# A pipeline of linear attention written out for all pairs of heads, and gate products placed in four column groups

## The chip, the cores and the metric

The kernel runs on one core of one Trainium2 chip. A core has TensorE (PE: matrix products, with a queue of its own for weight loads, PEld), VectorE (DVE), ScalarE (ACT), GpSimd (POOL) and SyncE (SP, which here only issues DMAs). The metric is device time in microseconds of the whole program, the median of several runs; lower is better. Durations come from one profiled execution.

## The reference

The input x is 4 sequences of 512 tokens with 256 channels, float32. Four layers are computed one after the other, each added to x:

```python
x = x + attn_a(layernorm(x))      # softmax attention, 16 heads of 16
x = x + ffn(layernorm(x))         # stage b
x = x + attn_b(layernorm(x))      # gated linear attention, 16 heads of 128
x = x + ffn(layernorm(x))         # stage d
```

The linear attention projects to q, k, v and a gate, runs a causal convolution with four taps over q and k, a silu and a layer norm for each head, and then the recurrence `S = (1 - b) S + b v k^T`, `o = S q`, which the kernel computes in blocks with a decay matrix:

```python
q = silu(causal_dwconv(h @ Wq)); k = silu(causal_dwconv(h @ Wk)); v = h @ Wv
q = layernorm(q); k = layernorm(k); b = sigmoid(h @ Wb + bb); gate = silu(h @ Wg)
# for every token t: S = (1 - b_t) S + b_t v_t k_t^T ; o_t = S q_t
out = (o * gate) @ Wo
```

The feed-forward layer picks two of eight routes for each token, and adds the token's result, times the route's gate, to **row number route** of the output. Only rows 0 to 7 of the first sequence get anything:

```python
h = silu(silu(x @ w1.T) @ w3.T) @ w2.T
for k in range(2):
    out = out.at[indices_k[:, k]].add(gates[:, k:k+1] * h)   # indices are 0..7
```

So the sum over tokens can be taken before the last product: gates^T (8 x 2048) times the hidden values (2048 x 256), and that times w2.

## The kernel before

The stages follow each other with a barrier of all engines between them: softmax attention, its projection, feed-forward b, layer norm and decay (c), linear attention, feed-forward d. Semaphores by hand order all work; nothing is scheduled by a tool.

**Linear attention** (`linear_attention`). Work goes by units: a unit is one head on one sequence. A pair of heads has `BODY` = 8 units, there are 8 pairs and 64 units. Each engine runs a function `step(pair, k, u, of)` for each unit, in which the phases of several units interleave: TensorE turns the normed q and k of unit u-2 back (L1340), projects q and k of unit u (L1306), turns the convolved rows of u-1 (L1333), projects the gate (L1306), computes scores of u-2 (L1325), the read-out of u-3 (L1392, L1389), projects values (L1319) and multiplies the gated rows of u-5 with Wo (L1414). DVE does the convolution steps (L1513), statistics (L1543), masks (L1518), the gated rows (L1563), values (L1569), the decay scans (L1522) and the sum into `x_tok` (L1532). ACT does the first tap, silu, norms and the high parts of split operands; POOL does the small sums of the norm and the low parts. SP loads the decay rows `keep` of each unit and, in a pair's second unit, the next pair's weights.

The helper `steps` writes the first two pairs out on every engine, and then a loop on the engine (`eng.Fori`) whose body is two pairs. With `last_apart` (SP, POOL, ACT, DVE) the loop runs for pairs 2 to 5, twice, and the last two pairs are written out; TensorE loops over pairs 2 to 7, three times. Within a loop the counts that `wait` (L1161) and `wait_apart` (L1167) wait for, and the columns of `par`, `beta_tok` and `wo` that depend on the head, come from registers that the engine's sequencer computes.

**Feed-forward** (`norm_and_ffn`, run for b and d). TensorE works out the router's logits (`rows`, 8 partitions, L773), turns them (L780), makes the upper products (L793) and the middle ones (L805); ACT writes the results of silu into `hidden_t` and `hidden`. DVE picks the two routes and makes the gates (L896 to L934). When `gates_ready` comes, TensorE multiplies, for each of the 16 token tiles, the gates (128x8) with `hidden` (128x256) into `rows`, L833. DVE copies that out (`summed`, L936), TensorE turns it with two transposes (L837), DVE copies (L938), TensorE multiplies with w2 (L841), DVE adds to `x_tok` (L940), and in d SP stores the eight rows. In b, POOL splits the weights of the first heads meanwhile (`ahead`).

A float32 product (not the split kind, float32r) shows as two passes with two weight loads in the trace: L833 is 16 products in the program and 32 in the trace.

## Time and profile before

| | |
|---|---|
| median of 3 runs | 1269.4 us (1269.29 to 1273.27) |
| the profiled execution | 1268.87 us |
| its span, first to last instruction | 1267.1 us |
| PE busy | 1172.9 us (93%) |
| DVE busy | 969.6 us (77%) |
| ACT busy | 758.1 us (60%) |
| POOL busy | 569.5 us (45%) |
| linear attention | 388.6 to 1209 us |
| feed-forward b, d | 316 to 375 us, 1209 to 1267 us |

Busy time counts no register, branch or semaphore instructions and no issuing of DMAs. Busy shares are means over stages with different limits, so they don't say what a stage waits for. Where TensorE is busy all the time, the distance from one unit's start to the next tells what it loses; in the timeline a number in brackets is idle time of that engine just before the row, and the name behind it is what ended it. Matmuls overlap: the start of one is about 0.12 (256 columns) or 0.23 us (512) after the last one's, though each takes longer.

### The profile page before, as it was taken

How to read it: one execution, taken by the hardware profiler on the slowest of the kernel's cores; microseconds unless marked ns; L12 is line 12 of the kernel's file. 1: busy time of each engine (PE TensorE's matmuls, PEld its weight loads, DVE VectorE, ACT ScalarE, POOL GpSimd, SP SyncE). 2: the span in 40 equal slices, each digit the busy share in tenths (PEclk: the TensorE clock that was granted, in tenths of full speed). 3: DMA queues.
4: the chain of work that ended last, by engine and by line, in shares of the span. 5: the costliest groups of instructions: out<-in, count | busy, mean ns of one | idle time of the engine just before them, and what ended most of it. 6: DMA issues, size and time to landing. Idle time of an engine off the chain costs nothing. (4 is left out here: it accounts for less than half of the span.)

```text
span 1267.1 us, 22205 instructions
## 1 busy us (share of the span) xinstructions
PE 1172.9 (93%) x7062; PEld 915.1 (72%) x7062; DVE 969.6 (77%) x2038; ACT 758.1 (60%) x1400; POOL 569.5 (45%) x1066
## 2 busy tenths in 40 slices
PE   4799999998787999999999999999999999999778
PEld 3343434335555889898998988898898999899655
DVE  6767677764625888888898898888898988989451
ACT  3156565674334676776766676676767676666323
POOL 5100000000711675676676675676576666656410
PEclk9589999999799999999999999999999999999889
DMA  4212222200301111102011111201110110101020
GB/s 148 66 43 52 54 47 58 50 17 1 116 1 65 39 38 59 39 26 72 27 38 39 59 39 29 71 26 39 59 39 27 72 38 27 38 26 39 1 67 1
DMA packets 26677, 56.66 MB, mean 45 GB/s; under 512 B 5367, under 2 KB 10359, under 8 KB 25399
## 3 DMA queue, kind: packets, MB, share of 16 engines
q1 hardware_dynamic: 26551, 55.11, 14.4%
q8 instruction: 63, 1.03, 0.3%
q14 instruction: 63, 0.52, 0.1%
HBM read 39.95 MB, written 2.29 MB: 33 GB/s over the span
## 5 line engine op out<-in xcount | busy, mean ns | idle before, releaser
L555 DVE TENSOR_REDUCE a_neg_max<-a_scores 128x1 f32<-128x512 f32 x236 | 154.9, 685 | 64.1 <-PE a_scores L359 63.9
L1513 DVE SCALAR_TENSOR_TENSOR l_conv<-l_proj_q,par,l_conv 128x511 f32<-128x511 f32 (+2 forms) x192 | 142.5, 742 | 55.2 <-ACT l_conv L1430 52.0
L497 ACT ACTIVATE a_probs<-a_scores_t 128x1024 f32<-128x1024 f32 x128 | 124.3, 1023 | 57.9 <-PE a_scores_t L374 56.8
L1436 ACT ACTIVATE l_conv<-l_conv,par 128x512 f32<-128x512 f32 x128 | 92.4, 723 | 101.4 <-DVE l_conv L1513 101.0
L1513 DVE SCALAR_TENSOR_TENSOR l_conv<-l_proj_k,par,l_conv 128x511 f32<-128x511 f32 (+2 forms) x192 | 142.9, 744 | 6.3 <-DVE l_conv L1513 0.6
L1522 DVE TENSOR_TENSOR_SCAN l_decay<-l_keep,l_diag 128x256 f32<-128x256 f32 (+1 forms) x256 | 146.1, 633 | 0.0
L1249 POOL TENSOR_TENSOR l_k_tok<-l_normed,k_norm 128x256 f32<-128x256 f32 x64 | 56.3, 880 | 157.9 <-ACT l_normed L1447 157.9
L86 POOL MEMSET ln_minus_half_b<- 128x4 f32 x1 | 0.1, 101 | 281.0 <-POOLq L611 281.0
L359 PE MATMUL a_scores<-a_k_stack,a_q_stack 48*128 48x512 f32 x236 | 108.7, 507 | 15.3 <-DVE a_neg_max L555 11.7
L359 PEld LDWEIGHTS a_scores<-a_k_stack,a_q_stack 48*128 48x128 f32 x236 | 42.7, 193 | 105.9 <-DVE a_neg_max L555 87.4
L1447 ACT ACTIVATE l_normed<-l_turn_q,l_shift,l_scale 128x128 f32<-128x128 f32 x256 | 96.3, 457 | 21.1 <-POOL l_shift L1241 21.1
L1239 POOL TENSOR_TENSOR l_scale<-l_small,l_minus_half 128x8 f32<-128x8 f32 x64 | 105.0, 1641 | 5.0
L1392 PE MATMUL l_outp<-l_masked,l_values 128*128 128x128 f32 (+1 forms) x512 | 105.8, 330 | 0.9 <-DVE x_tok L1532 0.9
L1447 ACT ACTIVATE l_normed<-l_turn_k,l_shift,l_scale 128x128 f32<-128x128 f32 x256 | 97.1, 480 | 0.0
L1280 POOL TENSOR_TENSOR l_gated_lo<-l_gated,l_gated_hi 128x512 fp32r<-128x512 f32 x64 | 82.2, 1285 | 9.9 <-ACT l_gated_hi L1470 9.9
L1319 PE MATMUL l_proj_gv<-head_hi,xn_hi 128*128 128x256 f32 x256 | 83.5, 326 | 2.1 <-ACT l_gate L1489 2.1
L1489 ACT ACTIVATE l_gate<-l_proj_gv 128x512 f32<-128x512 f32 x64 | 38.2, 597 | 77.7 <-PE l_proj_gv L1306 77.6
L374 PE MATMUL a_scores_t<-a_q_stack,a_k_stack 50*128 50x512 f32 x256 | 72.3, 447 | 6.5 <-DMA a_q_stack<-a_max_lo 5.5
L1414 PE MATMUL l_outp<-wo_hi,l_gated_hi 128*128 (+1 forms) x256 | 72.9, 285 | 4.9 <-DVE l_gated L1563 3.1
L1392 PEld LDWEIGHTS l_outp<-l_masked,l_values 128*128 128x128 f32 x512 | 73.1, 193 | 4.5 <-issue 1.0
L1569 DVE TENSOR_TENSOR l_values<-l_proj_gv,beta_tok 128x512 f32<-128x512 f32 x64 | 44.2, 691 | 39.3 <-PE l_proj_gv L1319 39.1
L1414 PE MATMUL l_outp<-wo_hi,l_gated_lo 128*128 (+1 forms) x256 | 71.6, 280 | 0.0
(292 smaller groups left out, 3429.8 us busy)
## 6 DMA issues: line engine op xcount, KB each, us to landing
l_keep<-keep_rows SPq DMA_DIRECT2D x64, 384.0 KB, 3.4
head_raw<-w_heads SPq DMA_DIRECT2D x8, 1024.0 KB, 6.4
a_q_stack<-a_dense_hi SPq DMA_DIRECT2D x64, 64.0 KB, 2.2
a_k_stack<-a_dense_hi SPq DMA_DIRECT2D x64, 64.0 KB, 2.2
x_tok<-x SPq DMA_DIRECT2D x4, 512.0 KB, 7.0
a_q_stack<-a_dense_lo SPq DMA_DIRECT2D x32, 64.0 KB, 2.2
a_k_stack<-a_dense_lo SPq DMA_DIRECT2D x32, 64.0 KB, 2.2
wo_raw<-w_o SPq DMA_DIRECT2D x1, 2048.0 KB, 11.6
```

Of the source, the lines that this page charges most:

```text
L359: pe.matmul(max_bank(g, j), half_rows(q_stack[i], e, STACK)[:, slot, t * P:(t + 1) * P], half_rows(k_stack[i], e, STACK)[:, slot, :], star ...
L497: act.activation(probs[:, n % 2, 2 * half:2 * half + 2, :], scores_t[half][:], ACT.Exp, scale=SOFT_SCALE).then_inc(probs_done, 1)
L555: dve.tensor_reduce(neg_max[:, g % 2, at:at + 1], max_bank(g, j), AX.X, ALU.max, negate=True).then_inc(max_done, 1)
L1239: pool.tensor_tensor(scale[:, i, :], small[:, 7, :], minus_half[:], ALU.pow).then_inc(scales_ready, 1)
L1280: pool.tensor_tensor(gated_lo[:, k % 4, :], gated[:], f32(gated_hi[:, k % 4, :]), ALU.subtract).then_inc(gated_lo_done, 1)
L1319: last = pe.matmul(proj_gv[:, t * PAIR:(t + 1) * PAIR], lhs, rhs, start=(j == 0), stop=(j == 3 * KD - 1))
L1392: last = pe.matmul(outp[:, i * P:i * P + WIDTH[i]], values[:, c % 2, i, e * DK:(e + 1) * DK], masked[:, m, START[i]:START[i] + WIDTH[i]], ...
L1414: last = pe.matmul(outp[:, t * D:(t + 1) * D], lhs, rhs, start=(j == 0), stop=(j == 5))
L1436: act.activation(conv[:, w, m, :], conv[:, w, m, :], ACT.Silu, bias=par[:, h, 2 * TAPS + w:2 * TAPS + w + 1]).then_inc(act_sem[w], 1)
L1447: last = act.activation(normed[:, w, t, :], turn[w][:, t * P:(t + 1) * P], ACT.Identity, scale=scale[:, m, j:j + 1], bias=shift[:, m, j:j ...
L1513: ins = dve.scalar_tensor_tensor(conv[:, w, m, s:], proj[w][:, 0:SEQ - s], par[:, h, tap:tap + 1], conv[:, w, m, s:], ALU.mult, ALU.add)
L1522: last = dve.tensor_tensor_scan(decay[:, START[i]:START[i] + WIDTH[i]], keep[:, r, i * P:i * P + WIDTH[i]], diag[:, 0:WIDTH[i]], 0.0, ALU. ...
```

## The change

**No loop in the linear attention.** `steps` calls `step` for all eight pairs in turn on every engine, so pair and unit are plain numbers: all counts that are waited for and all column offsets are constants. The work, its order on each engine and the semaphores stay.

**Gate products in four column groups.** The last gate sum is written into a new tile `slots`, 32 columns for each token tile, of which 8 hold the gates and 24 are zero (POOL zeroes the tile early). The product of token tile t writes to 32 output partitions that start at 32 x (t mod 4) of a PSUM bank `sums` with 128 partitions, in place of partitions 0 to 7; each group sums four tiles. DVE copies all 128 partitions, and in place of the two transposes TensorE multiplies with `fold` (128x8, ones where the partition is e, e+32, e+64 or e+96), which turns and adds the four groups in one. DVE makes `fold` from the unit matrix ahead of the routing. The router's logits use the first 8 partitions of `sums` as they did `rows`.

```diff
--- before.py
+++ after.py
@@ -715,13 +715,16 @@
         ratio = sb("ratio", [P, NT])
         total = sb("total", [P, NT])
         weight = sb("weight", [P, 2, NT])
-        gates = sb("gates", [P, 3, NT, NE])
-        summed = sb("summed", [NE, D])
+        gates = sb("gates", [P, 2, NT, NE])
+        slots = sb("slots", [P, NT, SLOT])
+        fold = sb("fold", [P, NE])
+        summed = sb("summed", [P, D])
         summed_t = sb("summed_t", [P, KD, NE])
         xt = [[psum(f"xt{k}", [P, SEQ]) for k in range(KD)]]
         up = [psum(f"up{i}", [P, SEQ]) for i in range(2)]
         mid = [psum(f"mid{i}", [P, 2, D]) for i in range(2)]
-        rows = psum("rows", [NE, SEQ])
+        sums = psum("sums", [P, SEQ])
+        rows = sums[0:NE, :]
         turned = psum("turned", [P, (NT + KD) * NE])
         logits_ps = turned[:, 0:NT * NE].rearrange("p (t e) -> p t e", e=NE)
         tail = turned[:, NT * NE:].rearrange("p (k e) -> p k e", e=NE)
@@ -729,10 +732,10 @@
 
         names = ("w_loaded", "rank_set", "w_hi_ready", "w_lo_ready", "router_done", "router_read", "logits_done", "route",
                  "gap_ready", "ratio_ready", "gates_ready", "up_done", "up_read", "mid_done", "mid_read", "acc_done",
-                 "summed_ready", "tail_done", "tail_read", "rows_done", "rows_added", "stored")
+                 "summed_ready", "tail_done", "tail_read", "rows_done", "rows_added", "stored", "slots_set", "fold_ready")
         (w_loaded, rank_set, w_hi_ready, w_lo_ready, router_done, router_read, logits_done, route,
          gap_ready, ratio_ready, gates_ready, up_done, up_read, mid_done, mid_read, acc_done,
-         summed_ready, tail_done, tail_read, rows_done, rows_added, stored) = (sem(n) for n in names)
+         summed_ready, tail_done, tail_read, rows_done, rows_added, stored, slots_set, fold_ready) = (sem(n) for n in names)
         block = ctx.enter_context(nc.Block())
 
         @block.sync
@@ -754,6 +757,7 @@
             ln.constants(pool)
             for g in range(NB):
                 ln.deviations(pool, g)
+            pool.memset(slots[:], 0.0).then_inc(slots_set, 1)
 
             for e in range(NE):
                 pool.memset(rank[:, e:e + 1], float(NE - e)).then_inc(rank_set, 1)
@@ -770,7 +774,7 @@
                     pe.wait_ge(router_read, g)
                 for k in range(KD):
                     for lhs, rhs in split_passes(w_in_hi[:, k, D:], w_in_lo[:, k, D:], xn_hi[:, k, tok], xn_lo[:, k, tok]):
-                        last = pe.matmul(rows[:], lhs, rhs, start=(j == 0), stop=(j == 3 * KD - 1))
+                        last = pe.matmul(rows, lhs, rhs, start=(j == 0), stop=(j == 3 * KD - 1))
                         j += 1
                 last.then_inc(router_done, 1)
 
@@ -830,11 +834,14 @@
             for t in range(NT):
                 if t % 2 == 0:
                     pe.wait_ge(mid_read, t // 2 + 1)
-                last = pe.matmul(rows[:, 0:D], gates[:, 2, t, :], hidden[:, t, :], start=(t == 0), stop=(t == NT - 1))
+                j = t % (P // SLOT)
+                last = pe.matmul(sums[j * SLOT:(j + 1) * SLOT, 0:D], slots[:, t, :], hidden[:, t, :],
+                                 start=(t < P // SLOT), stop=(t >= NT - P // SLOT))
             last.then_inc(acc_done, 1)
+            pe.wait_ge(fold_ready, 1)
             pe.wait_ge(summed_ready, 1)
             for k in range(KD):
-                last = pe.transpose(tail[:, k, :], summed[:, k * P:(k + 1) * P], ident[0:NE, 0:NE])
+                last = pe.matmul(tail[:, k, :], summed[:, k * P:(k + 1) * P], fold[:], start=True, stop=True)
             last.then_inc(tail_done, 1)
             pe.wait_ge(tail_read, 1)
             for k in range(KD):
@@ -851,7 +858,7 @@
                 act.wait_ge(router_done, g + 1)
                 if g >= 2:
                     act.wait_ge(logits_done, g - 1)
-                act.activation(logit_rows[:, g % 2, :], rows[:], ACT.Copy).then_inc(router_read, 1)
+                act.activation(logit_rows[:, g % 2, :], rows, ACT.Copy).then_inc(router_read, 1)
 
             copy_logits(0)
             ln.high_parts(act, 1)
@@ -891,6 +898,8 @@
                 if g + 2 < NB:
                     ln.statistics(dve, g + 2)
             ln.low_parts(dve, NB - 1)
+            dve.tensor_reduce(fold[:], ident[:].rearrange("p (j e) -> p e j", e=SLOT)[:, 0:NE, :], AX.X,
+                              ALU.add).then_inc(fold_ready, 1)
             dve.wait_ge(logits_done, NB)
             dve.wait_ge(rank_set, NE)
             dve.tensor_copy(logits[:], logits_ps).then_inc(route, 1)
@@ -931,9 +940,10 @@
                 dve.tensor_tensor(gates[:, pick, :, :], chosen[:, pick, :, :],
                                   weight[:, pick, :].unsqueeze(2).to_broadcast(wide), ALU.mult).then_inc(route, 1)
             dve.wait_ge(route, step + 5)
-            dve.tensor_tensor(gates[:, 2, :, :], gates[:, 0, :, :], gates[:, 1, :, :], ALU.add).then_inc(gates_ready, 1)
+            dve.wait_ge(slots_set, 1)
+            dve.tensor_tensor(slots[:, :, 0:NE], gates[:, 0, :, :], gates[:, 1, :, :], ALU.add).then_inc(gates_ready, 1)
             dve.wait_ge(acc_done, 1)
-            dve.tensor_copy(summed[:], rows[:, 0:D]).then_inc(summed_ready, 1)
+            dve.tensor_copy(summed[:], sums[:, 0:D]).then_inc(summed_ready, 1)
             dve.wait_ge(tail_done, 1)
             dve.tensor_copy(summed_t[:], tail).then_inc(tail_read, 1)
             dve.wait_ge(rows_done, 1)
@@ -1178,19 +1188,11 @@
 
             return not isinstance(u, int) or 0 <= u - lag < UNITS
 
-        def steps(eng, step, lags, last_apart=False):
-
-            for pair in range(2):
+        def steps(step, lags):
+
+            for pair in range(PAIRS):
                 for k in range(BODY):
-                    step(pair, k, pair * BODY + k, pair)
-            with eng.Fori(1, PAIRS // 2 - 1 if last_apart else PAIRS // 2) as couple:
-                for of in range(2):
-                    for k in range(BODY):
-                        step(2 * couple + of, k, couple * (2 * BODY) + (of * BODY + k), of)
-            if last_apart:
-                for of in range(2):
-                    for k in range(BODY):
-                        step(PAIRS - 2 + of, k, (PAIRS - 2 + of) * BODY + k, of)
+                    step(pair, k, pair * BODY + k, pair % 2)
             for k in range(lags):
                 step(PAIRS, k, UNITS + k, 0)
 
@@ -1208,7 +1210,7 @@
                     wait(sp, w_ready, 4 * pair)
                     sp.dma_start(w_raw[:], w_heads[bass.ds(pair + 1, 1)]).then_inc(w_loaded, 16)
 
-            steps(sp, step, 0, last_apart=True)
+            steps(step, 0)
 
         @block.gpsimd
         def _(pool):
@@ -1293,7 +1295,7 @@
                 if k in SPLIT_AT and has_next(pair):
                     low_weights(pair, of, k - SPLIT_AT[0])
 
-            steps(pool, step, 4, last_apart=True)
+            steps(step, 4)
 
         @block.tensor
         def _(pe):
@@ -1418,7 +1420,7 @@
             def head_of(head, e):
                 return head + e
 
-            steps(pe, step, 6)
+            steps(step, 6)
 
         @block.scalar
         def _(act):
@@ -1498,7 +1500,7 @@
                     wait(act, read_out, v - 1)
                     act.activation(state[:, k % 2, :], score_b[:, 2 * P:2 * P + DK], ACT.Copy).then_inc(state_done, 1)
 
-            steps(act, step, 4, last_apart=True)
+            steps(step, 4)
 
         @block.vector
         def _(dve):
@@ -1579,7 +1581,7 @@
                     scan(kk % 2, range(TPB)).then_inc(decay_done, 1)
 
             dve.wait_ge(consts_set, 4)
-            steps(dve, step, 7, last_apart=True)
+            steps(step, 7)
 
 
 def build(nc, x, w_qkv, w_proj, b_proj, w_in, w_mid, w_out, w_beta, b_beta, w_heads, w_o, params, norms, k_norms, out):
```

The lines of the changed kernel are numbered a little higher than before (L1340 is L1342, L1513 is L1515, L833 is L838, L837 is L844).

TensorE at the end of the loop's body before: the products with Wo, then a register step and the branch back to the body's start, where the transposes of the normed q stand.

```order
L1414 MATMUL l_outp<-wo_hi,l_gated_hi 128x256
L1414 MATMUL l_outp<-wo_lo,l_gated_hi 128x256
L1414 MATMUL l_outp<-wo_hi,l_gated_lo 128x256
L1186 REGISTER_ALU
L1186 COMPARE_AND_BRANCH
```

The same place in the changed kernel:

```order
L1416 MATMUL l_outp<-wo_hi,l_gated_hi 128x256
L1416 MATMUL l_outp<-wo_lo,l_gated_hi 128x256
L1416 MATMUL l_outp<-wo_hi,l_gated_lo 128x256
L1342 MATMUL l_turn_q<-ident,l_normed 128x128 x4
L1308 MATMUL l_proj_q<-xn_hi,head_hi 128x512
L1308 MATMUL l_proj_q<-xn_lo,head_hi 128x512
```

The products and the transposes follow each other directly; register step and branch are gone.

DVE in the loop before, from one unit's sum into `x_tok` on (`ISA` and `REGISTER_ALU` are register instructions of the sequencer, which compute a column offset or a count):

```order
L1161 REGISTER_ALU
L1532 TENSOR_TENSOR x_tok<-l_outp,x_tok 128x512
L1161 REGISTER_ALU
L1513 ISA
L1513 SCALAR_TENSOR_TENSOR l_conv<-l_proj_q,par,l_conv 128x511
L1161 ISA
L1513 ISA
L1513 SCALAR_TENSOR_TENSOR l_conv<-l_proj_q,par,l_conv 128x510
L1161 ISA
L1543 BN_STATS l_stats<-l_turn_q 128x6 x4
L1543 BN_STATS l_stats<-l_turn_k 128x6 x4
L1161 REGISTER_ALU
```

The same unit's work in the changed kernel:

```order
L1534 TENSOR_TENSOR x_tok<-l_outp,x_tok 128x512
L1515 SCALAR_TENSOR_TENSOR l_conv<-l_proj_q,par,l_conv 128x511
L1515 SCALAR_TENSOR_TENSOR l_conv<-l_proj_q,par,l_conv 128x510
L1545 BN_STATS l_stats<-l_turn_q 128x6 x4
L1545 BN_STATS l_stats<-l_turn_k 128x6 x4
L1515 SCALAR_TENSOR_TENSOR l_conv<-l_proj_q,par,l_conv 128x509
```

The vector work and its order are the same, without register instructions in between.

TensorE at the end of stage d, before and then changed:

```order
L805 MATMUL f_mid_d<-w,f_hidden_t_d 128x256 x16
L833 MATMUL f_rows_d<-f_hidden_d,f_gates_d 8x256 x16
L837 MATMUL f_turned_d<-ident,f_summed_d 128x8 x2
L841 MATMUL f_rows_d<-w,f_summed_t_d 8x256 x2
```

```order
L809 MATMUL f_mid_d<-w,f_hidden_t_d 128x256 x16
L838 MATMUL f_sums_d<-f_hidden_d,f_slots_d 32x256 x16
L844 MATMUL f_turned_d<-f_fold_d,f_summed_d 128x8 x2
L848 MATMUL f_sums_d<-w,f_summed_t_d 8x256 x2
```

The gate products write 32 partitions instead of 8, and the transposes of `summed` with `ident` are products of `summed` with `fold`.

## Rows read from the trace of the kernel before

**Rows 1.** Page, head: the span of the profiled execution.

```profile
span 1267.1 us, 22205 instructions
```

**Rows 2.** Busy time by stretch: us, busy of each engine (count), granted clock, DMA.

```profile
578.00:777.00 199.00, 198.58 (x1296) 179.34 (x1295) 174.92 (x371) 139.24 (x286) 131.06 (x248) 1.00 0.13 44
```

**Rows 3.** Timeline, PE: first projection product of units 8, 16, 17, 32, 48, 63.

```profile
482.36 0.48 PE L1306 MATMUL l_proj_q<-xn_hi,head_hi 128*128 128x512 f32 x1
...
580.33 0.48 PE L1306 MATMUL l_proj_q<-xn_hi,head_hi 128*128 128x512 f32 x1
...
593.25 0.48 PE L1306 MATMUL l_proj_q<-xn_hi,head_hi 128*128 128x512 f32 x1
...
779.84 0.47 PE L1306 MATMUL l_proj_q<-xn_hi,head_hi 128*128 128x512 f32 x1
...
979.09 0.47 PE L1306 MATMUL l_proj_q<-xn_hi,head_hi 128*128 128x512 f32 x1
...
1162.80 0.48 PE L1306 MATMUL l_proj_q<-xn_hi,head_hi 128*128 128x512 f32 x1
```

**Rows 4.** PE at the back edges; then queue instructions of line L1186: min/median/max.

```profile
777.29 0.27 PE L1414 MATMUL l_outp<-wo_hi,l_gated_lo 128*128 x1
779.43 0.65 PE L1340 MATMUL l_turn_q<-ident,l_normed 128*128 128x128 f32 x4 [1.87 <-issue]
...
978.68 0.65 PE L1340 MATMUL l_turn_q<-ident,l_normed 128*128 128x128 f32 x4 [1.65 <-issue]
...
L1186 PEldq COMPARE_BRANCH  x3: 83/3288/3501, 775.8 to 1173.0; - x3
```

**Rows 5.** Timeline, DVE and PE: convolution steps in loop, written out; a product with Wo.

```profile
587.83 1.64 DVE L1513 SCALAR_TENSOR_TENSOR l_conv<-l_proj_k,par,l_conv 128x510 f32<-128x510 f32 x2 [0.15 <-DVE l_conv L1513]
...
985.29 2.30 DVE L1513 SCALAR_TENSOR_TENSOR l_conv<-l_proj_k,par,l_conv 128x511 f32<-128x511 f32 x3
...
591.37 0.38 PE L1414 MATMUL l_outp<-wo_hi,l_gated_hi 128*128 x1 [0.39 <-DVE l_gated L1563]
```

**Rows 6.** Timeline: tail of stage d, gate products and what stands around them.

```profile
1255.37 0.29 DVE L934 TENSOR_TENSOR f_gates_d<-f_gates_d 128x128 f32<-128x128 f32 x1
1255.42 1.08 ACT L875 ACTIVATE f_hidden_d<-f_mid_d 128x512 f32<-128x512 f32 x2
1255.72 7.07 PE L833 MATMUL f_rows_d<-f_hidden_d,f_gates_d 128*8 128x256 f32 x32 [0.32 <-DVE f_gates_d L934]
1262.83 0.41 DVE L936 COPY f_summed_d<-f_rows_d 8x256 f32<-8x256 f32 x1 [7.16 <-PE f_rows_d L833]
...
1263.30 0.28 PE L837 MATMUL f_turned_d<-ident,f_summed_d 8*128 8x8 f32 x2 [0.51 <-DVE f_summed_d L936]
```

**Rows 7.** Timeline: gate products of stage b, and POOL behind the barrier.

```profile
365.03 7.07 PE L833 MATMUL f_rows_b<-f_hidden_b,f_gates_b 128*8 128x256 f32 x32 [0.32 <-DVE f_gates_b L934]
...
375.91 0.30 POOL L978 MEMSET d_zeros<- 16x256 f32 x1 [24.32 <-POOLq L1631]
```

**Rows 8.** Timeline, PE: a context product of softmax attention; its line, min/median/max ns.

```profile
122.63 1.07 PE L391 MATMUL a_ctx_acc<-a_probs,a_v_tok 128*32 128x512 f32 x8
123.62 0.49 PE L359 MATMUL a_scores<-a_k_stack,a_q_stack 48*128 48x512 f32 x2
...
L391 PE MATMUL a_ctx_acc<-a_probs,a_v_tok x512: 589/617/1061, 63.3 to 295.5; 128*32 128x512 f32 x171
```

**Rows 9.** Timeline: a four-pass product, a copy from PSUM, DVE ahead of routing.

```profile
574.98 0.61 PE L1373 MATMUL l_score_b<-l_values,l_k_tok 128*128 128x128 f32 x4
...
386.33 0.39 DVE L1035 COPY beta_tok<-d_turned 128x256 f32<-128x256 f32 x1
...
1245.55 0.29 DVE L896 COPY f_logits_d<-f_turned_d 128x128 f32<-128x128 f32 x1 [10.04 <-PE f_turned_d L780]
```

**Rows 10.** DMA queues, the larger one for instructions: packets, MB, share of engines.

```profile
q8 instruction: 63, 1.03, 0.3%
```

**Rows 11.** Busy time by stretch, near the end of the linear attention.

```profile
1190.00:1195.00 5.00, 5.00 (x20) 4.46 (x19) 1.12 (x2) 0.28 (x1) 1.12 (x1) 0.51 0.00 0
```

## The prediction

> **What bounds the kernel now.** I read the span and the busy shares first, then the busy time of each engine in two pairs of the linear attention, then when TensorE starts each unit, then the rows around the places that the edit touches. The span is 1267.1 us and the profiled execution 1268.87 us, so 1.8 us lie outside the span [rows 1]. In the linear attention TensorE is busy 198.58 of 199 us at the full clock, DVE 174.92, ACT 139.24 and POOL 131.06 [rows 2]. So here the end is set by TensorE, and what counts is the time that TensorE loses, not what others save.
>
> What it loses is read from the start of each unit's first projection product. Units 8 to 16 start at 482.36 and 580.33: 97.97 us for 8, or 12.246 each. Units 48 to 63 start at 979.09 and 1162.80: 183.71 for 15, or 12.247 each [rows 3]. That is the undisturbed pace, the same in the first two pairs, which every engine has written out, and in the last two, where only TensorE still loops. Between them it is worse: units 16 to 32 take 779.84 - 580.33 = 199.51 us and units 32 to 48 take 979.09 - 779.84 = 199.25, where 16 units at that pace take 195.95.
>
> In the two feed-forward stages TensorE works alone at one place: the 16 gate products, which run as 32 passes one behind the other in 7.07 us, while DVE waits 7.16 for them and ACT has nothing after 1256.50 [rows 6]. It is the chain to the end in stage d, and to the barrier in stage b, where POOL had by then waited 24.32 us [rows 7].
>
> **The change, part 1: no loop.** It removes what lies between 195.95 and the measured: 199.51 + 199.25 - 2 x 195.95 = **6.86 us**, and I can name what it consists of.
> - The two taken back edges. From the last product of the loop's body to the next pass 777.29 to 779.43 = 2.14 us go by, where such products follow each other in 0.12; TensorE is idle 1.87 and at the second edge 1.65 [rows 4]. TensorE's queue spends 3288 and 3501 ns on the branch (median and longest of three; the third, 83 ns, is the one that falls through), of which the queued products hide the rest. The first edge costs 2.14 - 0.12 = 2.02, the second 0.22 less by its idle row, 1.80: together 3.8 us.
> - The late vector work. In the loop DVE has register instructions ahead of each convolution step, and 0.15 us go by idle between two of them (587.83); in the last two pairs three run on without a gap (985.29). So DVE ends its chain later, and TensorE waits for the gated values: 0.39 us at 591.37, in a unit that takes 593.25 - 580.33 = 12.92 instead of 12.25 [rows 3, 5]. It comes at the first units of a pair, 0.25 to 0.67 us at a time, eight times: the rest, 3.0 us.
>
> What is late next when both are gone? Nothing, as far as 23 units with DVE, ACT and POOL written out show (8 to 15, and 48 to 62): they hold 12.25 each. The one thing that these rows don't cover is TensorE without a loop after unit 16. Bounds: at least the branches, 3.8; at most 7.5, since the first units of each pair could have been held even at 12.25. I take 6.9. Queue instructions (register work on all queues) go too; TensorE's engine doesn't feel them. No DMA is moved: SP issues the same transfers on the same counts.
>
> The row on the branch meets two pages of the Trainium skill. "Advanced Engine Details and Errata", Control Flow Timing, gives about 108 ns for a compare-and-branch: by that the back edge would hide wholly behind queued products and this part would be worth 3.0. "Runtime: NRT & Kernel Launch", Instruction fetch mechanics, says that a taken branch to a target outside the small window of fetched pages has to fetch it first: by that the whole 3.8 is gone. The trace agrees with the second (3288 ns).
>
> **Part 2: gate products in four column groups.** Sixteen products, two passes each, now go to four groups of 32 output partitions. The only such work in the trace is the context product of the softmax attention: 8 passes of 512 columns in 1.07 us from the first start to the last end, one pass 0.589 at least, so the last starts 0.48 after the first, where two rounds of four start 0.46 apart plus a skew of 0.02 [rows 8]. Passes of four groups therefore do run side by side, a round of 512 columns taking 0.46. For 256 columns: one pass behind the other is (7.07 - 0.38) / 31 = 0.216 [rows 6]; a round is 0.23 (half of 0.46) to 0.25 (0.216 plus the 0.03 by which a 512-column round exceeds two passes of 0.216). I take 0.24. Eight rounds: 7 x 0.24 + 0.02 + 0.38 = 2.1 us. Saved: 7.07 - 2.1 = **5.0 us** per stage. The upper bound is that, the lower nothing, if groups don't overlap here.
> - Does another wait take its place? The last quarter needs ACT's last gated rows, at 1255.42 + 1.08 = 1256.50. It would start at 1255.72 + 6 x 0.24 = 1257.2 [rows 6]. So no, with 0.7 us to spare.
> - The two transposes of 0.28 us become two 128-row products with the fold matrix, four passes with 128-column weights. Nearest rows: four passes of 128x128 in 0.61 [rows 9]; the transposes themselves, 0.28 [rows 6]. So +0 to +0.33; I take +0.3, since the weights are as wide as in the row of 0.61.
> - The copy out of PSUM has 128 partitions instead of 8: 0.39 for 128x256 against 0.41 [rows 6, 9]. Nothing.
> - The fold sum on DVE is one small reduction just ahead of a wait of 10.04 us [rows 9]: hidden. DVE waits for one more semaphore ahead of the last gate sum, long given, and writes in strides: 0 to 0.1, taken as 0. The zeroing on POOL (512 columns; 256 took 0.30 [rows 7]) stands ahead of the rank constants and, in b, of the weight split that ended 24 us before the barrier: hidden; without that cover some 0.6.
>
> Per stage 5.0 - 0.3 = 4.7, two stages **9.4 us**. Bounds -0.8 to 10.
>
> "TensorEngine Tiling (Array Packing)" of the Trainium skill, Key Properties, speaks against this part: changing the tiling mode drains TensorE. The trace shows how little: the plain products start 123.62, that is 1.0 after the first of the grouped passes and before the last ends, and here DVE's copy stands behind the switch anyway. By the rule the sum stays as it is, within 0.2.
>
> **Sum.** 6.9 + 9.4 = 16.3. 1268.9 - 16.3 = 1252.6 for a profiled execution; that one stood 0.5 under the median of 1269.4, so **1253.1 us**.
>
> **Rivals.**
> - The clock moves. The changed tails shift everything behind them, and stretches at 1.2 GHz (0.51 granted at 1190 to 1195 [rows 11]) follow idle ones. Such a stretch of 5 us costs 2.5, one half as long 1.25. One more: 1254.4 to 1255.6. One less: 1250.6 to 1251.9. The start of the linear attention and both feed-forward tails are places for it. Against much more: TensorE is at 1.00 through all of the middle [rows 2].
> - Only the branch was the loop's doing, and the slow first units of a pair have another cause: 1253.1 + 3.0 = 1256.1. Against: units 48 to 63 have none.
> - The groups don't overlap for these products, the change does not do what it says: 1253.1 + 2 x 5.0 = 1263. Against: [rows 8], the same types and rows; only half the columns and back-to-back quarters are new.
> - Slower: straight code has to be fetched too. The larger queue for instructions moved 63 packets in the span [rows 10]; the six pairs that the edit writes out take 595 of 1267 us, so by their share some 30. If each stalled TensorE, the change loses from 16.3 / 30 = 0.54 us each on; at the 1.9 us of a back edge it would be 1253 + 57 = 1310. Against: units 8 to 16 and every loop body are straight code, and show 12.246.
>
> **How the numbers follow.** Forecast as summed 0.68; a low clock stretch more 0.10, one less 0.08; slow units stay 0.06; groups don't overlap 0.05; fetch stalls 0.03. The range takes in both clock cases, the slow units and the bounds of the pass costs (0.5 either way): 1249.8 to 1257.2. About 0.3% is what a measurement of this kernel can tell from no change (4 us). Faster by more holds in all but fetch stalls: 0.96; within 0.3% 0.02, half of a mild fetch case; slower 0.02.
>
> **What would show it.** Right: no branch in TensorE's queue, no idle row of 1.87 or 1.65; units 16 to 48 in 391.9 us instead of 398.8; DVE's convolution steps without the 0.15; the 32 gate passes in 2.1 us in one row, DVE's wait before the copy about 2.2; the fold products at 0.6. Wrong if a unit after the 16th takes over 12.3, if the gate passes take over 3 us, or if a stretch with a low clock appears where none was.

## The result

The changed kernel takes 1253.7 us in the median (1252.24 to 1254.71), beside 1269.35 us for the kernel before (1269.02 to 1273.27): 0.987 of the time, with a 95% interval from 0.985 to 0.989. The forecast was 1253.1. The profiled execution after is 1253.70 us against 1268.87.

The page's head, and the stretch of the linear attention that [rows 2] shows of before (us, busy time of each engine with its count, granted clock, DMA share, GB/s):

```profile
span 1251.7 us, 21457 instructions
```

```profile
578.00:777.00 199.00, 199.00 (x1301) 180.23 (x1300) 178.31 (x375) 139.99 (x284) 131.90 (x252) 1.00 0.14 45
```

TensorE now has no idle time in these 199 us. The first projection products of units 16 and 48, to be read as [rows 3]:

```profile
576.46 0.48 PE L1308 MATMUL l_proj_q<-xn_hi,head_hi 128*128 128x512 f32 x1
...
968.35 0.48 PE L1308 MATMUL l_proj_q<-xn_hi,head_hi 128*128 128x512 f32 x1
```

They are 391.89 us apart, or 12.247 a unit; before it was 979.09 - 580.33 = 398.76. From unit 6 on no unit is over 12.3 (a unit's time here is the distance from the start of the unit ahead of it to its own). DVE's two convolution steps over k now run on without the 0.15 us of [rows 5]:

```profile
582.66 1.52 DVE L1515 SCALAR_TENSOR_TENSOR l_conv<-l_proj_k,par,l_conv 128x511 f32<-128x511 f32 x2
```

The tail of stage d, to be held against [rows 6]:

```profile
1244.68 0.29 DVE L944 TENSOR_TENSOR f_slots_d<-f_gates_d 128x128 f32<-128x128 f32 x1
1244.72 1.09 ACT L882 ACTIVATE f_hidden_d<-f_mid_d 128x512 f32<-128x512 f32 x2
...
1245.03 1.93 PE L838 MATMUL f_sums_d<-f_hidden_d,f_slots_d 128*32 128x256 f32 x32 [0.32 <-DVE f_slots_d L944]
1247.03 0.42 DVE L946 COPY f_summed_d<-f_sums_d 128x256 f32<-128x256 f32 x1 [2.06 <-PE f_sums_d L838]
...
1247.60 0.58 PE L844 MATMUL f_turned_d<-f_fold_d,f_summed_d 128*128 128x8 f32 x4 [0.64 <-DVE f_summed_d L946]
1248.22 0.17 DVE L948 COPY f_summed_t_d<-f_turned_d 128x16 f32<-128x16 f32 x1 [0.77 <-PE f_turned_d L844]
```

The 32 passes take 1.93 us instead of 7.07, and from their start to the end of the span it is 1251.7 - 1245.03 = 6.67 instead of 1267.1 - 1255.72 = 11.38. ACT's last gated rows are there at 1245.81, before the last quarter needs them. The same in stage b, where [rows 7] has 365.03 and 375.91:

```profile
364.60 1.93 PE L838 MATMUL f_sums_b<-f_hidden_b,f_slots_b 128*32 128x256 f32 x32 [0.32 <-DVE f_slots_b L944]
...
370.80 0.30 POOL L988 MEMSET d_zeros<- 16x256 f32 x1 [19.00 <-POOLq L1633]
```

From the gate products to the work behind the barrier it is 6.20 us instead of 10.88.

**Where 0.9 us of the expected gain went.** The gain in the span is 15.4 us, where 16.3 were summed. Two windows of the kernel after, and then two of the kernel before, at the same work (the end of stage c and the first unit of the linear attention), differ in the granted clock, the column behind the busy times:

```profile
382.00:388.00 6.00, 4.14 (x10) 3.30 (x11) 0.34 (x2) 0.69 (x1) 0.52 (x4) 0.51 0.57 151
388.00:398.00 10.00, 8.64 (x46) 7.08 (x45) 6.96 (x13) 5.20 (x7) 0.00 (x0) 0.95 0.24 98
```

```profile
387.00:393.00 6.00, 4.41 (x13) 3.50 (x13) 1.25 (x2) 0.69 (x1) 0.51 (x4) 0.72 0.57 187
393.00:403.00 10.00, 8.29 (x45) 6.48 (x43) 7.05 (x17) 5.52 (x8) 0.00 (x0) 1.00 0.18 76
```

The first row of each pair holds the end of TensorE's wait of 2.9 us for the barrier and the first products of unit 0. After, the clock stands at the lower level, 1.2 GHz, in all of it (0.51) and into the second; before, only through a part of the first (0.72). POOL's row behind b's barrier came 375.91 - 370.80 = 5.11 us earlier than before, unit 0 (383.86 against 388.59) 4.73, unit 6 (453.99 against 457.87) 3.88: 1.2 us of what b had saved are gone. Up to b's gate products the execution was 0.43 ahead. So 0.43 + 4.68 - 1.23 + 6.87 + 4.71 = 15.46, the 15.4 of the spans within rounding.

### The profile page after: what moved, and what is told of

Its sections match the earlier page's. It is cut to its first block and busy times, and to the rows that moved or that the text cites. A ratio compares the mean times of both kernels' runs of the same rounds, so it can differ in the third digit from the quotient of the medians.

```text
span 1251.7 us, 21457 instructions
## 1 busy us (share of the span) xinstructions
PE 1160.6 (93%) x7066; PEld 911.4 (73%) x7066; DVE 971.9 (78%) x2040; ACT 758.5 (61%) x1400; POOL 565.9 (45%) x1068
## 5 line engine op out<-in xcount | busy, mean ns | idle before, releaser
L1515 DVE SCALAR_TENSOR_TENSOR l_conv<-l_proj_q,par,l_conv 128x511 f32<-128x511 f32 (+2 forms) x192 | 142.5, 742 | 48.8 <-ACT l_conv L1432 46.5
L1515 DVE SCALAR_TENSOR_TENSOR l_conv<-l_proj_k,par,l_conv 128x511 f32<-128x511 f32 (+2 forms) x192 | 142.9, 744 | 4.6
L1251 POOL TENSOR_TENSOR l_k_tok<-l_normed,k_norm 128x256 f32<-128x256 f32 x64 | 52.1, 815 | 158.3 <-ACT l_normed L1449 158.3
L1416 PE MATMUL l_outp<-wo_hi,l_gated_hi 128*128 128x256 f32 x256 | 72.0, 281 | 4.1 <-DVE l_gated L1565 2.3
L1416 PE MATMUL l_outp<-wo_hi,l_gated_lo 128*128 128x256 f32 x256 | 71.7, 280 | 0.0
```

The lines of the kernel that those rows point to most:

```text
L1416: last = pe.matmul(outp[:, t * D:(t + 1) * D], lhs, rhs, start=(j == 0), stop=(j == 5))
L1515: ins = dve.scalar_tensor_tensor(conv[:, w, m, s:], proj[w][:, 0:SEQ - s], par[:, h, tap:tap + 1], conv[:, w, m, s:], ALU.mult, ALU.add)
```

## The experiments

The first is the kernel before with one half of the edit; all others are edits of the changed kernel, and those of the second part give single engines their loop back. No kernel leaves a part of the computation out. To free the comparison from what lies ahead of stage b, which moves by some microseconds from kernel to kernel (below), the profiled time less the start of b's gate products is used: 903.84 before, 889.10 after, -14.74. The time for units 16 to 48, from rows like those above, is called the middle.

The kernels on single engines and on the order of the groups ran once each, so of their whole times only large differences can be read:

| run | whole time | start of b's gate products | from there on |
|---|---|---|---|
| the changed kernel | 1253.70 | 364.60 | 889.10 |
| pe_loop | 1259.53 | 366.76 | 892.77 |
| short_branch | 1256.63 | 366.90 | 889.73 |
| dve_loop | 1255.40 | 365.94 | 889.46 |
| act_loop | 1251.73 | 363.36 | 888.37 |
| dve_act_loop | 1253.96 | 364.62 | 889.34 |
| four_loops | 1255.06 | 365.49 | 889.57 |
| two_groups | 1257.55 | 367.04 | 890.51 |
| groups_in_runs | 1264.58 | 369.62 | 894.96 |

The time from b's gate products on isn't steady either: from unit 63 to the gate products of stage d, with the same code, these nine take between 91.15 and 92.98 us. So the readings below rest on the middle and on single rows.

### Each half alone

**The loops gone, the gate products as before.**

```diff
-            steps(pe, step, 6)
+            steps(step, 6)
...
                 last = pe.matmul(rows[:, 0:D], gates[:, 2, t, :], hidden[:, t, :], start=(t == 0), stop=(t == NT - 1))
```

> The linear attention is written out on all engines, the feed-forward stages are those of before. Theory (the two halves are independent and add up): units 16 to 48 of TensorE take 391.9 us instead of 398.8, the gate products stay at 7.07 us, and the time is 1269.4 - 6.9 = 1262.5. Rival (the written-out code gives part back elsewhere, for example by fetching): over 1264, with units over 12.3 us after unit 16.

Measured: 1263.12 us (1261.85 to 1265.12), 0.9946 of the kernel before (0.9921 to 0.9972). Timeline, TensorE: units 16 and 48, and the gate products of d:

```profile
581.41 0.48 PE L1298 MATMUL l_proj_q<-xn_hi,head_hi 128*128 128x512 f32 x1
...
973.30 0.48 PE L1298 MATMUL l_proj_q<-xn_hi,head_hi 128*128 128x512 f32 x1
...
1249.99 7.07 PE L833 MATMUL f_rows_d<-f_hidden_d,f_gates_d 128*8 128x256 f32 x32 [0.32 <-DVE f_gates_d L934]
```

The middle is 391.89, as after. From b's gate products on the kernel takes 897.08: -6.76. The whole time, 0.6 over the 1262.5 expected, is still below the 1264 of the rival, and no unit after the sixteenth is over 12.3.

**The column groups, the loops as before.**

```diff
-            steps(step, 6)
+            steps(pe, step, 6)
...
                 last = pe.matmul(sums[j * SLOT:(j + 1) * SLOT, 0:D], slots[:, t, :], hidden[:, t, :],
...
```

> Gate products in four column groups, the linear attention with its loops as before. Theory: gate products 1.93 us in both stages, the linear attention keeps its idle rows of 1.87 and 1.65 at the back edges, time 1269.4 - 9.4 = 1260.0; up to 1.2 more if the start of the linear attention again has a longer stretch at 1.2 GHz, as in the changed kernel. Rival (the clock stretch comes from the loop half): then no longer stretch here and 1260.0 sharp.

Measured: 1261.02 us (1258.53 to 1263.29), 0.9927 (0.9903 to 0.9951). From b's gate products on 895.89: -7.95. With the loops' -6.76 that is -14.71, where both together have -14.74: the halves add up. (That they do so within 0.03 is luck in part. From unit 63 to d's gate products these four kernels happen to agree, 92.86 to 92.99.) The gate passes take 1.93 in both stages. The middle has its loop losses again, 975.93 - 576.96 = 398.97, the second back edge among them (timeline, TensorE):

```profile
576.96 0.48 PE L1316 MATMUL l_proj_q<-xn_hi,head_hi 128*128 128x512 f32 x1
...
975.52 0.65 PE L1350 MATMUL l_turn_q<-ident,l_normed 128*128 128x128 f32 x4 [1.75 <-issue]
975.93 0.47 PE L1316 MATMUL l_proj_q<-xn_hi,head_hi 128*128 128x512 f32 x1
```

The two windows at the start of the linear attention have the clock of the kernel after, not that of before:

```profile
382.00:388.00 6.00, 3.65 (x9) 2.91 (x10) 0.48 (x2) 0.66 (x1) 0.51 (x4) 0.56 0.48 118
388.00:398.00 10.00, 8.63 (x45) 7.00 (x44) 6.75 (x10) 5.24 (x8) 0.00 (x0) 0.92 0.29 118
```

So in these four kernels the 1.2 us go with this half: 2 x 4.7 less 1.2 is 8.2, and 7.95 are measured, with 0.2 of the rest in the middle (398.97 where the kernel before has 398.76). Kernels further down don't all keep to that.

### What the loop cost: which engine's

The kernels of this part give some engines the loop of the kernel before back, as `looped`, and leave the others written out.

**TensorE alone.**

```diff
-            steps(step, 6)
+            looped(pe, step, 6)
```

> The changed kernel, but TensorE alone runs pairs 2 to 7 in a loop, as before. Theory (the back edges cost 3.8 us, and the slow first units of a pair come from the other engines' register work): units 32 and 48 start 14.3 and 14.1 us after the one ahead, all others hold 12.25, time 1253.7 + 3.8 = 1257.5. Rival (TensorE's own registers make the slow units): units 17, 18, 25, 26 and so on take 12.5 to 12.9 too, 1260.6.

Measured: the middle is 397.56. Timeline of TensorE at the first back edge, windows around it, and the branch in TensorE's queue (minimum, median, maximum in ns):

```profile
774.20 0.27 PE L1432 MATMUL l_outp<-wo_hi,l_gated_lo 128*128 x1
776.36 0.69 PE L1358 MATMUL l_turn_q<-ident,l_normed 128*128 128x128 f32 x4 [1.88 <-issue]
776.77 0.71 PE L1324 MATMUL l_proj_q<-xn_hi,head_hi 128*128 128x512 f32 x1
```

```profile
770.00:776.00 6.00, 4.48 (x34) 4.12 (x32) 5.31 (x10) 3.80 (x10) 2.65 (x4) 1.00 0.03 5
776.00:781.00 5.00, 4.64 (x18) 3.83 (x19) 1.23 (x3) 2.52 (x4) 2.84 (x4) 0.66 0.19 67
781.00:787.00 6.00, 6.00 (x39) 5.35 (x38) 5.58 (x15) 2.31 (x5) 2.94 (x10) 1.00 0.04 15
```

```profile
L1196 PEldq COMPARE_BRANCH  x3: 83/3298/3515, 772.7 to 1170.2; - x3
```

Units 32 and 48 take 14.34 and 14.19, 4.03 more than 2 x 12.25; all others hold 12.25 but unit 33, with 13.84. That one goes with the clock, which stands at 0.66 from 776 to 781, right behind the idle 1.88 us. Whether that idle time brought the low clock is not shown: at the same edge of the kernel before, behind 1.87 us, the clock stays at 1.00 (779.5 to 784), and so it does here behind the second edge (976 to 980). So the edges alone cost 4.0, and the other slow units of [rows 3, 5] don't come from TensorE's loop alone.

**The branch without the distance.** TensorE has no loop over the work, but branches back twice over a single empty instruction at the same two places.

```diff
+                if short and pair in (4, 6):
+                    with short.Fori(0, 2) as turn:
+                        short.nop(nofuse=True)
```

> The changed kernel, with an empty loop of two turns put into TensorE's program ahead of pairs 4 and 6: two taken branches to a target a few instructions back. Theory (the 3.3 us of the branch are the fetch of a target far away): no idle of TensorE, 1253.7. Rival (any taken branch costs that much): TensorE is idle 1.6 to 1.9 us at units 32 and 48, 1257.5.

Measured: the middle is 391.89 with no idle time. The branch in TensorE's queue:

```profile
L1195 PEldq COMPARE_BRANCH  x4: 76/148/362, 774.0 to 970.3; - x4
```

The two taken ones need 219 and 362 ns, a branch with the same instruction over a whole loop body 3298 and more. It is the distance that costs, not the branch or the counter. One of the queues that move instructions agrees, which moves more where the target is far: 57 packets in the changed kernel, 63 with TensorE's loop alone, 58 with the short branch (page, DMA queues; packets, MB, share; pe_loop, then short_branch):

```profile
q8 instruction: 63, 1.03, 0.3%
```

```profile
q8 instruction: 58, 0.95, 0.3%
```

"Advanced Engine Details and Errata" of the Trainium skill, Control Flow Timing, gives some 108 ns for a compare-and-branch: the near ones here take 76 to 362 ns, the taken ones two to a little over three times that figure, and the far ones some thirty times. "Runtime: NRT & Kernel Launch", Instruction fetch mechanics, has a far target fetched first, and the trace agrees with it as far as these two kernels go.

**DVE alone; ACT alone; both; all but TensorE.**

```diff
-            steps(step, 7)
+            looped(dve, step, 7, last_apart=True)
```

> The changed kernel, but DVE alone loops over pairs 2 to 5, as before. Theory (DVE's register instructions ahead of each convolution step make the gated values late): the first two units of pairs 2 to 5 take 12.5 to 12.9 us again, 3.0 us in all, time 1256.7, with gaps of 0.15 us between convolution steps. Rival (ACT's registers do it): all units hold 12.25, 1253.7.

Measured: the middle is 971.44 - 577.86 = 393.58, 1.7 more, not 3.0. The same eight units as before are slow (17, 18, 25, 26, 33, 34, 41, 42), but at 12.39 to 12.46, with 12.69 once (34). The gaps are back (timeline, DVE):

```profile
585.23 1.64 DVE L1531 SCALAR_TENSOR_TENSOR l_conv<-l_proj_k,par,l_conv 128x510 f32<-128x510 f32 x2 [0.15 <-DVE l_conv L1531]
```

```diff
-            steps(step, 4)
+            looped(act, step, 4, last_apart=True)
```

> The changed kernel, but ACT alone loops over pairs 2 to 5, as before. Theory (DVE is the one that makes units slow): all units of TensorE hold 12.25 us, 1253.7. Rival (ACT's register work, 0.05 to 0.09 us ahead of its activations, makes DVE's chain late): the first two units of pairs 2 to 5 take 12.5 to 12.9, 1256.7.

Measured: 391.89 and no slow unit. ACT's register instructions alone cost nothing.

```diff
+            looped(act, step, 4, last_apart=True)
...
+            looped(dve, step, 7, last_apart=True)
```

> The changed kernel, but DVE and ACT both loop over pairs 2 to 5, as before. With DVE alone in a loop units 16 to 48 took 393.59 us, with ACT alone 391.89, written out 391.89, and the kernel before owed 3.0 us to its slow first units. Theory (DVE's and ACT's register work lie one behind the other on the chain from the first tap to the gated values, and ACT's shows only once DVE's has used the slack up): 394.9 us. Rival (the missing 1.3 us are POOL's or SP's registers): 393.6 us.

Measured: 394.17, 2.3 more; the eight units take 12.50 to 12.57. ACT's loop costs 0.6 where DVE is late too, and nothing without it. That reads like two chains that feed each other, each with a little slack; the slack itself was not measured.

```diff
+            looped(sp, step, 0, last_apart=True)
...
+            looped(pool, step, 4, last_apart=True)
...
+            looped(act, step, 4, last_apart=True)
...
+            looped(dve, step, 7, last_apart=True)
```

> The changed kernel, but SP, POOL, ACT and DVE loop over pairs 2 to 5, as before, and TensorE alone is written out. DVE and ACT in loops took 394.17 us for units 16 to 48, 0.7 short of the 3.0 that the slow units cost before, and it is units 17 and 33 that are short (12.57 and 12.55 instead of 12.91 and 12.87). Theory (POOL's or SP's register work brings the rest, at the first unit of an iteration): 394.8 us, units 17 and 33 at 12.9, time about 1256.6. Rival (TensorE's own loop brings it): 394.2 us, units 17 and 33 at 12.6, 1256.0.

Measured: 394.31, 2.4 more, with 12.57 at unit 17 and 12.65 at 33. With the column groups alone, where TensorE loops as well, these two take 12.90 and 12.89. So SP and POOL add 0.1. The middle of these four loops and the edges of TensorE's give 394.31 + 4.03 = 398.34, where the two kernels in which all five loop have 398.76 and 398.97: 0.4 to 0.6 are left that show only when TensorE loops with the others; neither TensorE alone nor the other four have them. What passes between them there stays open.

### The gate products: why 1.93

**Two groups in place of four.**

```diff
-                j = t % (P // SLOT)
+                j = t % 2
```

> The changed kernel with two column groups instead of four (even token tiles to partitions 0 to 31, odd ones to 32 to 63; copy and fold use 64 partitions). Theory (a round of passes of all groups takes one pass plus about 0.01 to 0.03 us, whatever the number of groups): 16 rounds of 0.22 to 0.23, so 3.6 to 3.9 us for the 32 passes in place of 1.93, and per stage 1.8 us more: 1253.7 + 3.6 = 1257.3. Rival (the passes are bound by the writing of results, not by the array): two groups take as long as four, 1253.7.

Measured (timeline, TensorE):

```profile
1247.46 3.65 PE L838 MATMUL f_sums_d<-f_hidden_d,f_slots_d 128*32 128x256 f32 x32 [0.32 <-DVE f_slots_d L944]
...
1251.72 0.58 PE L844 MATMUL f_turned_d<-f_fold_d,f_summed_d 64*128 64x8 f32 x4 [0.61 <-DVE f_summed_d L946]
```

Sixteen rounds of two: (3.65 - 0.38) / 15 = 0.218 a round, beside 0.216 for one pass alone [rows 6] and (1.93 - 0.38 - 0.02) / 7 = 0.219 for a round of four. With one, two or four groups a round costs what one pass costs. The fold of two groups takes the 0.58 us of four.

**Four groups, each filled before the next.** The four tiles of a group follow each other, where the changed kernel goes round the groups.

```diff
-                j = t % (P // SLOT)
+                j = t // (P // SLOT)
```

> The changed kernel, but token tiles 0 to 3 go to the first column group, 4 to 7 to the second and so on, in place of going round. Theory (products start in program order, so one that waits for its busy group holds up the next group's): hardly anything overlaps, the 32 passes take about 6.5 us, and the time is 1253.7 + 2 x 4.6 = 1262.9. Rival (each group has a queue of its own, since passes of four products start ahead of their second passes): 1.93 us as now, 1253.7.

Measured (timeline, TensorE):

```profile
1253.54 4.59 PE L838 MATMUL f_sums_d<-f_hidden_d,f_slots_d 128*32 128x256 f32 x32 [0.32 <-DVE f_slots_d L944]
```

That is neither the 7.07 of one behind the other (nor the 6.5 expected of a strict order) nor 1.93: theory and rival both miss. The passes start 0, 0.24, 0.46, 0.67, 0.89, 0.90, 1.11, 1.14, 1.32 and 1.35 us after the first, and so on in pairs up to the last four, which are single again: 4 + 12 x 2 + 4 = 32 passes in 20 steps, 19 x 0.22 + 0.38 = 4.6 us. The rows don't name the group of a pass. If passes of one group stay 0.22 apart, as before, the next group's first pass starts together with the fifth of the eight passes of the group ahead, while three passes that the program has before it have yet to start. So the order of starts isn't strictly that of the program, but the overlap reaches only a little way ahead in it, and never more than two passes start together. What limits it was not tried. "TensorEngine Tiling (Array Packing)" of the Trainium skill, Key Properties, says that tiles work independently of each other; that holds here only for products that stand near each other in the program.

### Can more be had

**The clock kept up in stage c.** Eleven products that nobody reads are added at its end, where TensorE of the changed kernel waits 2.86 us for the barrier.

```diff
+            for i in range(11):
+                pe.matmul(xt[0][i % 2][:], ident[:], ident[:], start=True, stop=True)
```

> The changed kernel, with 11 products of 128x128 that nobody reads behind the last transposes of stage c, where TensorE otherwise idles up to the barrier (about 2.4 us of 3). They take no real work's place. Theory (the idle time there is what brings the stretch of 6.8 us at 1.2 GHz at the start of the linear attention): the stretch goes or halves, units 0 to 6 take 68.5 us or less instead of 70.1, time 1252.2 or less. Rival (that stretch comes from what is ahead of or behind it): units 0 to 6 stay at 69.3 to 71, time 1253.7, or 0.3 more if the barrier comes later.

Measured: 1252.66 us (1249.87 to 1255.46), 0.9878 (0.9853 to 0.9904), which cannot be told from the changed kernel. Windows from the end of stage c on:

```profile
383.00:389.00 6.00, 5.70 (x35) 4.86 (x35) 1.47 (x4) 1.13 (x2) 0.51 (x4) 1.00 0.47 110
389.00:403.00 14.00, 9.27 (x54) 7.38 (x52) 11.89 (x24) 7.57 (x12) 3.56 (x10) 1.00 0.22 88
403.00:408.00 5.00, 4.13 (x15) 3.42 (x16) 0.49 (x2) 3.49 (x10) 2.53 (x4) 0.66 0.02 9
...
418.00:421.00 3.00, 3.00 (x11) 2.41 (x10) 0.35 (x1) 2.10 (x5) 2.31 (x4) 0.50 0.00 0
```

The start is at the full clock now, and unit 1 follows unit 0 by 7.31 us where it was 9.62. But TensorE then waits for its data (busy 9.27 of 14 us), and a low stretch comes that the changed kernel doesn't have: unit 4 takes 13.14 where it took 11.58. Units 0 to 6 take 69.37 in all, beside 70.13 after: 0.8 come back by this profile. That is short of the 68.5 of the theory and lies in the rival's range.

**The gates' exponential one step earlier.** ACT computes the gates' ratio one pair of tiles earlier, so that the gates are ready before the last middle products.

```diff
-                        if n == NT // 2 - 2:
+                        if n == NT // 2 - 3:
```

> The changed kernel, with ACT's exponential for the gates (and its two table loads of 1.28 us) one product of the middle layer earlier: ahead of the sixth of eight instead of the seventh. With the gate products down to 1.93 us, ACT's last rows are the next thing on the chain. Theory (the gates are ready 1.7 us earlier, the gate products start as hidden rows come and end some 0.5 us after the last of them): 0.3 to 0.6 us less per stage, 1252.5 to 1253.1. Rival (the middle products have only two buffers and wait for ACT, which loads tables: the last one comes 0.6 us later): nothing gained or 0.5 lost per stage, 1253.7 to 1254.7.

Measured: 1256.73 us (1255.34 to 1256.98), 0.9909 (0.9891 to 0.9927): slower than the changed kernel. Timeline of TensorE:

```profile
1240.34 5.34 PE L809 MATMUL f_mid_d<-w,f_hidden_t_d 128*128 128x256 f32 x24
1246.45 1.97 PE L809 MATMUL f_mid_d<-w,f_hidden_t_d 128*128 128x256 f32 x8 [0.76 <-ACT f_hidden_d L882]
1248.34 1.93 PE L838 MATMUL f_sums_d<-f_hidden_d,f_slots_d 128*32 128x256 f32 x32
```

The wait of 0.32 us for the gates is gone, but ACT, which changes its function table twice for the exponential (1.28 us each time), now keeps the last middle products waiting for 0.76. From the first middle pass to the end of the gate passes it is 9.93 us, where the changed kernel has 9.33 (it starts at 1237.63): 0.6 lost in each stage. The distance of the whole kernels lies elsewhere. By the profiles the two kernels are 3.05 us apart, and the first product of that middle pass in stage b comes 3.83 us later (361.04 against 357.21), behind code that is the same in both. From there on this kernel is even 0.8 ahead, in spite of the 1.2 lost: 0.84 come back in units 0 to 6 (69.29 beside 70.13) and 0.74 between unit 63 and stage d's middle products (84.84 beside 85.58), where the code is the same. So the loss of 0.6 a stage is shown, and the 3.0 between the medians is not the edit's price. A window of the softmax attention of this kernel, and then of the changed one:

```profile
45.00:90.00 45.00, 37.78 (x128) 16.43 (x126) 28.38 (x49) 15.11 (x19) 0.00 (x0) 0.62 0.20 46
```

```profile
45.00:90.00 45.00, 37.45 (x153) 16.67 (x153) 30.90 (x53) 17.16 (x23) 0.00 (x0) 0.73 0.23 54
```

The clock stands lower, 128 passes go through where there were 153, and b's gate products start at 369.04 instead of 364.60.

## Why the prediction was right, and where it was not

**What bounds the kernel.** TensorE in the middle, as read from the unit starts: giving back what it lost against the undisturbed pace gave all of it, and nothing was late behind it. Idle time would have told less: between 560 and 990 us the kernel before has 3.5 us of it at the back edges and 0.7 in front of products with Wo, 4.2 of the 6.87; the rest is hidden in rows that count as busy. The forecast of 6.86 us from the distance to the undisturbed pace came out at 6.87. The bound for a new fetch cost in straight code is settled too: the units hold 12.247 all through, and the two queues for instructions moved less than before, not more (page, DMA queues, to be held against [rows 10]; packets, MB, share):

```profile
q8 instruction: 57, 0.93, 0.3%
q14 instruction: 52, 0.43, 0.1%
```

**The back edges.** Summed at 3.8, measured alone at 4.0. The short branch shows that it is the distance of the target.

**The late vector work.** The size of 3.0 was right, being the rest of a measured distance, but its explanation is the step that failed in part: "in the loop DVE has register instructions ahead of each convolution step" carries 1.7 of it. ACT's registers carry 0.6 together with DVE's, SP's and POOL's 0.1, and some 0.5 need TensorE's loop as well. The row of 0.39 us in front of a product with Wo named DVE as what released TensorE; that names the last link, not the chain behind it. It did no harm to the number since all loops went at once. For a change to DVE's loop alone the same working would have forecast 3.0 and found 1.7.

**The gate products.** Summed at 2.1 with a round of 0.24, measured 1.93 with 0.219. The estimate had been drawn from a round of 512 columns, whose price above two passes of 256 was carried over in full; at 256 columns hardly any of it shows. The way back costs a little more than the 0.3 taken: from the start of the first copy to that of the second it was 0.79 and is 1247.03 to 1248.22 = 1.19, 0.1 of it since the copy's end and the fold's start lie 0.1 further apart. The two misses cancel: 4.7 a stage was forecast, 4.68 and 4.71 came. That other waits don't take its place held as well, DVE waiting 2.06 (2.2 were forecast) and ACT ready in time.

**The clock.** It was a rival and not in the sum, with 1.25 for a stretch half as long, and at the place named, the start of the linear attention. It came at about that size, 1.2. What brings it stays open. Units 0 to 6 take 69.3 us in the kernel before, with the loops gone alone and with two groups; 70.1 to 70.2 in the changed kernel, with the four groups alone and in the five kernels that give loops back. But with the exponential earlier they take 69.29, in spite of the four groups, and with the short branch 71.04, though its code up to there is the changed kernel's; with the groups filled one after the other it is 71.03. So it goes with the column groups in most kernels, not in all, and the same code gives more than one size of it. That the time at which the idle places come decides is a guess; it was not tried by itself. That the median missed by only 0.6 is luck in part: 0.43 were gained ahead of stage b, where nothing was changed, and the 0.5 by which the profiled execution before lay under its median was not there after.

**The other rivals.** That the groups don't overlap fell to [rows 8]'s reading, and the run with filled groups shows how near it lay: the same products in another order would have given 4.59, and the edit some 5 us less in all. That only the branch was the loop's doing fell to the pace. Slower by fetching fell to the queues.

## What to carry to other kernels

Measure a loop on an engine by the pace of what is written out beside it, and expect a far back edge (here 2 us each, behind queued products) and, on engines that feed the bounding one, register work between dependent instructions as two costs apart. Where single products with few output partitions run alone, spread them over column groups and go round the groups in the order of the program; then sum what folds the groups together again. And name a low-clock stretch as a possible term where the work ahead of an idle place gets shorter: here one took back an eighth of the tails' gain.

## What was unexpected in the hardware

- A round of four column groups costs no more than one pass (0.219 against 0.216 us for 256 columns), but only with the groups in turn. Filled one after the other, never more than two start together, and the same 32 passes take 4.59 us instead of 1.93.
- A taken branch over one instruction needs 0.2 to 0.4 us in TensorE's queue, and none shows on the engine; over a loop body 3.3 to 3.5, of which 1.65 to 1.97 show as idle. Once the idle of such an edge was followed by a stretch at the lower clock that cost another 1.6 us; at the same edge in the kernel before it was not.
- Kernels with the same code up to stage b reach its gate products between 363.36 and 369.62 us. The granted clock in the softmax attention goes with it: the nine with 0.73 from 45 to 90 us reach them at 363.36 to 366.04, the five with 0.61 to 0.70 at 366.76 to 369.62. So one profiled execution can't tell 3 us in the whole. It tells a few tenths in a stretch at the full clock, such as the middle; from unit 63 to d's gate products the same code takes 91.0 to 93.0.
